# Moving the last three of eight elementwise subtractions per pair from VectorE to GpSimd in a fused embedding, attention and FFN kernel

## The reference, cut to what matters

```python
h = patches @ tokW + tokb, joined with rows of the text table   # 192 tokens per sequence
h = h + attention(layernorm(h))                                 # causal, one head of 256
h = h + ffn(layernorm(h))
# ffn: x_norm = x / rms(x); up to 1024 with ternary weights (-1, 0, 1); exact gelu;
#      again x / rms(x); down to 256 with ternary weights
```

## Time and profile before

| what | value |
|---|---|
| median of 3 runs | 1138.72 us (1138.6 to 1143.58) |
| profiled execution, its own time | 1146.54 us |
| profiled execution, span from first to last instruction | 1144.7 us |
| busy in the span: PE, PEld | 968.9 us (85%), 849.7 us (74%) |
| busy in the span: DVE, ACT, POOL | 895.5 us (78%), 568.8 us (50%), 473.1 us (41%) |
| DMA, mean over the span | 84 GB/s |

### The profile page before, as it was taken

One profiled execution on the slowest core, in us unless ns is written; L12 is line 12 of the kernel. 1 busy time (PEld: TensorE's weight loads), 2 busy tenths in 40 slices (PEclk: granted clock), 3 DMA queues, 4 the chain that ended last, 5 costly groups with the idle time before them and its releaser, 6 DMA issues. The chain is left out here.

```text
span 1144.7 us, 19447 instructions
## 1 busy us (share of the span) xinstructions
PE 968.9 (85%) x5806; PEld 849.7 (74%) x5806; DVE 895.5 (78%) x2534; ACT 568.8 (50%) x1110; POOL 473.1 (41%) x602
## 2 busy tenths in 40 slices
PE   2378799999999999875789999999999999963886
PEld 2377688888888888774367788888888888752776
DVE  1667788888888888865137899998999998854997
ACT  1034555555555555552255577666666766612331
POOL 2124444444444444332023455554454454424443
PEclk9589899999999999986779999999999999955989
DMA  3111111111111110002169999999999999944110
GB/s 133 60 61 38 37 40 41 37 37 37 37 37 37 37 37 25 15 21 85 66 63 119 139 154 151 160 156 133 152 163 152 147 161 125 134 67 142 49 56 19
DMA packets 133534, 96.05 MB, mean 84 GB/s; under 512 B 9672, under 2 KB 127568, under 8 KB 132944
## 3 DMA queue, kind: packets, MB, share of 16 engines
q1 hardware_dynamic: 131920, 90.93, 52.1%
q0 software_dynamic: 1536, 4.20, 1.2%
HBM read 31.66 MB, written 13.11 MB: 39 GB/s over the span
## 5 line engine op out<-in xcount | busy, mean ns | idle before, releaser
L285 POOL TENSOR_TENSOR gelu_lo<-gelu_out,gelu_hi 128x384 fp32r<-128x384 f32 x80 | 87.8, 1105 | 98.8 <-DVE gelu_hi L435 98.8
L562 PE MATMUL psA<-x2T_hi,ternary_up 128*128 128x384 f32 x256 | 92.7, 362 | 11.0 <-ACT gelu_out L351 7.3
L609 PE MATMUL psA<-ternary_down,gelu_hi 128*128 128x256 f32 x384 | 99.0, 295 | 3.2 <-POOL gelu_lo L285 3.2
L846 POOL TENSOR_TENSOR B_decayed_u<-B_scan_in 128x512 f32<-128x512 f32 x48 | 62.1, 1293 | 86.6 <-DMA B_scan_in<-B_stage 79.9
L609 PE MATMUL psA<-ternary_down,gelu_lo 128*128 128x256 f32 x384 | 96.6, 289 | 0.0
L562 PE MATMUL psA<-x2T_lo,ternary_up 128*128 128x384 f32 x256 | 86.0, 336 | 0.0
L1096 PE MATMUL psB<-Win_hi,B_x_hi 128*128 128x512 f32 x192 | 84.3, 439 | 0.0
L834 POOL TENSOR_TENSOR B_y<-B_scan_in,B_states 128x512 f32<-128x512 f32 x48 | 62.0, 1291 | 52.1 <-ACT B_states L901 52.1
L1106 PEld LDWEIGHTS psB<-B_partial_dots,B_minus_same_batch 128*128 128x128 f32 x384 | 67.1, 196 | 21.9 <-DVE B_partial_dots L992 13.6
L1008 DVE SCALAR_TENSOR_TENSOR psB<-B_decayed_u,psB 128x128 f32<-128x128 f32 x192 | 68.0, 354 | 16.0 <-PE psB L1106 15.7
L609 PEld LDWEIGHTS psA<-ternary_down,gelu_hi 128*128 128x128 f32 x384 | 75.9, 198 | 4.4 <-POOL gelu_lo L285 3.9
(11 more groups left out here) (251 smaller groups left out, 3448.4 us busy)
## 6 DMA issues: line engine op xcount, KB each, us to landing
B_scan_in<-B_stage SPq DMA_DIRECT2D x192, 256.0 KB, 7.8
patches<-in_patches SPq DMA_DIRECT2D x16, 384.0 KB, 3.1
B_residual<-layer_out SPq DMA_DIRECT2D x48, 128.0 KB, 5.5
out_dram<-B_residual SPq DMA_DIRECT2D x48, 128.0 KB, 4.6
C_raw<-in_experts SPq DMA_DIRECT2D x8, 768.0 KB, 4.3
layer_out<-residual SPq DMA_DIRECT2D x32, 128.0 KB, 1.8
layer_out<-residual SPq DMA_DIRECT2D x32, 64.0 KB, 2.0
weight_stage<-in_upT SPq DMA_DIRECT2D x1, 1024.0 KB, 5.6
```

What stands on the lines that cost most here:

```text
L285: nc.gpsimd.tensor_tensor(act_l[:, k, :], act[:, k % DEEP, :], act_h[:, k, :].bitcast(F32), ALU.subtract).then_inc(s["ffn_lo"], 1)
L562: last = nc.tensor.matmul(out, a, b, start=(n == 0), stop=(n == len(terms) - 1))
L609: last = nc.tensor.matmul(ps[:, 6 + k // 2, (k % 2) * D:(k % 2 + 1) * D], x[:, c, k * P:(k + 1) * P], dn_w[:, c, :], start=(c == 0 and x i ...
L846: nc.gpsimd.tensor_tensor(lu[:, j % 2], ring[:, j % R_RING, :, LAM, :], ring[:, j % R_RING, :, U, :], ALU.mult).then_inc(s["lu"], 1)
```

## The change

`lo_vector`, the chunks whose low part VectorE makes, becomes empty, so `lo_pool` holds all eight. The instructions at L438 vanish, GpSimd runs L285 three more times per pair, and every wait in `wait_lo` counts on GpSimd's semaphore alone.

```diff
-        lo_vector = (3, 5, 7)
+        lo_vector = ()
         lo_pool = [k for k in range(FC) if k not in lo_vector]
```

## The result

The changed kernel takes 1128.2 us (median of 14 runs, 1120.99 to 1134.47) against 1141.36 for the kernel before (14 runs, 1133.55 to 1146.65). The ratio is 0.989, 95% interval 0.9864 to 0.9915: 1.1% faster. The changed kernel was measured once more on another occasion, with 0.986 (0.9819 to 0.9902). The profiled execution takes 1132.51 us with a span of 1130.7. Forecast were 1125.0 against 1138.72, a ratio of 0.988. The change saves 13.2 us, 13.75 forecast. That 1128.2 lies just above the forecast's own range of 1122 to 1128 comes from the kernel before, which took 2.6 us more in these 14 runs than in the first three. Ratios leave out the executions that took over 1.5% more than the fastest of their kernel, two of ten in the run with chunks 3 and 5 alone (its profile is of one of them) and two of thirteen of the kernel before in the set with (1, 2, 3, 5).

The account below looks back on a forecast made before the run. VectorE was taken to set the pace from chunk 3 on, TensorE following. 14 steps x 1.0 + 0.75 - 1.0 = 13.75 us off the median 1138.72 gave 1125.0; own range 1122 to 1128, overall 1119 to 1140, leaving out h1 held.

Parts of the forecast that it names:

- The bound: In part A's regular pairs, VectorE sets the pace from chunk 3 on and TensorE follows it.
- Whoever asks first holds the other: VectorE and GpSimd reading SBUF: first runs; after release the other needs 0.87 (GpSimd), 0.42 (subtraction or addition), 0.21 us (cast).
- Slot 3: Addition 2, cast 4 and `xT_lo` on VectorE: neither gains nor loses; 0.56 saved and 0.21 pause pay for blocked cast.
- the four places: Trace spots showing VectorE and GpSimd holding each other: low part 7, an addition, the `x_normed` behind it, a cast.
- Chunk 7 just in time: GpSimd finishes chunk 7 at 277.1, TensorE needs it at 277.25: 0.1 us to spare; GpSimd's pause hides the moved work.
- Next to nothing left over: TensorE at x2T gains 1.0 us; VectorE is late next, by some 0.1 us per pair.
- More: Rival, chance 0.05: casts never wait behind GpSimd, TensorE's room caps the gain at 1.44 us per pair: 1119 us.
- The last two pairs: Pair before the last gains 0.75 us at h1; last pair loses 1.0 as TensorE waits for GpSimd's chunk 7.
- 15 steps of 28.1 us: Part A's pairs are regular by `rms_mean`, 106.8 to 528.8 us; one pair's reading stands for 14 full steps.
- GpSimd asks first: Rival, chance 0.16: GpSimd's request holds additions 2 and 3, h1 only 0.56 us earlier per pair: 1131.8 us.
- The blocks eat it all: Rival, chance 0.12: GpSimd's chunk 6 slips between casts 6 and 7, h1 gains nothing: 1139.9 us.
- h1 held: Rival, chance 0.15: h1's scalar counts as a second SBUF read, GpSimd holds h1, 0.53 us late per pair: 1147.9 us.

Follow-up runs that it names:

- 3 and 5 alone: Changed kernel, but chunk 7's low part stays on VectorE, so only chunks 3 and 5 move to GpSimd; ratio to the kernel before 1.0095.
- (1, 2, 3, 5): Changed kernel, but VectorE makes the low parts of chunks 1, 2, 3 and 5; 1119.3 us, ratio 0.9822; repeated 1120.2 us, 0.9821.
- 7 alone: Changed kernel, but low parts 3 and 5 stay on VectorE, so only chunk 7's moves to GpSimd; 1126.15 us, ratio 0.9875.
- GpSimd made late: Changed kernel plus one unused subtraction of the same size on GpSimd right ahead of chunk 7's low part; ratio to the kernel before 0.9899.
- (3, 5, 6, 7): Changed kernel, but VectorE makes the low parts of chunks 3, 5, 6 and 7; ratio to the kernel before 1.0014.
- (2, 3, 5): Changed kernel, but VectorE makes the low parts of chunks 2, 3 and 5, GpSimd the other five; 1122.57 us, ratio 0.9818.

## Why the prediction was right

**The bound.** VectorE sets the pace from chunk 3 on, TensorE follows. The waits for `tT_lo` and `x_normed` L535 went when VectorE's chain got shorter, and that for L494, ahead of chunk 3, stayed at 9.7 us. Shown.

**Whoever asks first holds the other.** The rule held wherever the sum depends on it. It failed at cast 4, where the sum does not (next paragraph). The forecast of 0.21 (cast) and 0.87 (GpSimd) behind a release came out: cast 6 ends at 270.21, 0.23 after GpSimd's chunk 5 (269.98), and that chunk ends 0.86 after addition 3 (269.12). The runs with 7 alone and with 3 and 5 alone gave 26.88 and 28.44 for 26.9 and 28.4. So the two parts of the sum are shown by themselves, +1.30 for chunk 7 and -0.29 for chunks 3 and 5: the whole gain of the change comes from chunk 7, and the other two take 0.27 of it back. That chunk 3 has 0 of this and chunk 5 the rest is read from the trace, not from a run of each: `xT_lo` starts 1.89 behind cast 3, 1.90 before.

**Slot 3.** The total of 0 was right, and the way to it was not. Cast 4 was to be held until 272.15, since chunk 3 had asked first, and passed instead; so the rule taken from the four places is not complete. The forecast stood because `xT_lo` waits for ScalarE either way. Chunk 4 starts 1.92 behind cast 3, 1.98 forecast, which is luck: it was to wait for a held cast 4, and it waited for a chunk 3 that ended late. Cast 5 is held by 0.04 instead of 0.08.

**Chunk 7 just in time.** Forecast 6.85 us behind cast 3, measured 6.84 (272.33 - 265.49). That any lateness would stall TensorE one for one holds for down.0 and not for the period: with chunk 7 about 1 us late the period rose by 0.26.

**What is late next.** "Next to nothing left over" at x2T was too small a room. I took the score matmuls at 2.26 us to the next slot, and with `x_normed` ready they take 2.15, so TensorE still waits 0.17 for `x_normed` in each pair, 0.04 forecast. Behind it comes the wait ahead of ss, which I counted (0.35) for the rival *More* and not here; it measures 0.41. Neither touched the forecast, which VectorE's chain sets.

**The last two pairs** were mis-sized, at -0.25 us together. The steps of `rms_mean` there are 26.08 for 27.49 and 20.33 for 19.49: +1.41 - 0.84 = 0.57. The last one's 1.0 of loss is 0.84. In the pair before it, cast 3 to h1 takes 5.56 for 6.29, a gain of 0.73 as forecast (0.75); the other 0.66 comes from TensorE's clock (last section), which the sum had at nothing.

**The steps.** The sum was 14 x 1.0 - 0.25 = 13.75. The "15 steps of 28.1 us" are a mean over unequal ones: 36.94, twelve of 28.0 to 28.2, 27.49 and 19.49. The twelve middle steps gave 1.0 to 1.04 each, 12.2 together. The one ahead of them gave 0.65 (36.94 to 36.30); it holds a wait of TensorE of some 7 us behind ScalarE, which waits for the transfer of a weight. For the first pair no gain shows: its `rms_mean` stands at 106.8 in both, but over all traces it lies anywhere between 103.4 and 108.5, so that the trace cannot tell. The sum from first to last is 13.45. That the total came so near to 13.75 is in part luck: the regular pairs gave 1.1 less than 14.0, the last two 0.8 more than -0.25.

**The rivals.** GpSimd asks first: no, both additions took 0.55. The blocks eat it all: no, cast 7 ran through behind a held cast 6 (1.44 for both). More: in part, cast 4 did not have to wait, and it brought nothing, as VectorE then waited 0.81 for `xT_hi`. h1 held: no, 0.47 over GpSimd's chunks 6 and 7. One scalar per partition and one tile from SBUF, with the other tile from PSUM, were not held by GpSimd here. The Trainium skill, "SBUF — State Buffer", section "Who interferes with whom", frees instructions with at most one SBUF input, outside the two-port modes, and leaves open whether a scalar counts as one; by this trace it does not.

## What to carry to other kernels

Where two engines hold each other up, counting instructions is not enough; count meetings too, that is, instructions of the two that overlap in time and hold each other. Moving work pays most where the moved instruction stood behind the other engine, and costs where the one that follows it will stand there. Read in order of time which instructions are longer than their shortest form, and what ran beside them: here taking away one subtraction of 1.25 us, 0.69 of it waiting, brought 1.30 per pair, more than the whole gain. A replay of one regular pair from measured starts and ends, with the rule of who waits taken from four places of the same trace, gave the period to 0.02 us here, and to 0.04 in the runs with 7 alone and with 3 and 5 alone. It did less well where other things than VectorE's chain counted or the rule was stretched: 26.55 for 26.4 in the run with (1, 2, 3, 5), and 27.42 for 28.1 where GpSimd was made late.

## What the runs showed of the hardware

In the pair before the last, 0.66 of the 1.41 us gained goes with where TensorE's clock was low. A window over x2T and ss (length, busy times with counts, granted clock, DMA), in the kernel before, behind a wait of 4.15 us for `x_normed`:

```profile
506.60:509.30 2.70, 2.64 (x13) 2.64 (x14) 1.03 (x3) 1.04 (x2) 0.00 (x0) 0.50 0.00 0
```

and in the changed kernel, first over down.0 and down.1 behind three waits for GpSimd (0.49, 0.84 and 0.46 us), then over x2T and ss, behind a wait of 0.95 us:

```profile
488.00:492.00 4.00, 3.72 (x18) 3.46 (x18) 2.48 (x11) 0.00 (x0) 2.29 (x4) 0.61 0.00 0
```

```profile
492.90:495.00 2.10, 1.76 (x13) 1.52 (x14) 1.07 (x4) 1.08 (x2) 0.00 (x0) 1.00 0.00 0
```

In the kernel before the clock was at its lower level (1.2 GHz, 0.50) just where the end of the pair hangs on TensorE. In the changed kernel the low stretch (0.61 in the mean) came earlier, in matmuls whose end nobody waited for, and the clock was full (2.4 GHz, 1.00) over x2T and ss. From x2T to `rms_mean` it took 2.65 us (506.66 to 509.31) and then 1.99 (492.99 to 494.98): 0.66 of the 1.41 us gained in that pair. The second trace of the changed kernel shows the same (2.00), and so do the runs with 7 alone and with GpSimd made late. With 3 and 5 alone and with (3, 5, 6, 7) it is 2.65 at the low clock, but so it is with (2, 3, 5), where chunk 7 is on GpSimd too. That the earlier small waits moved the low stretch is my reading; it was not tried by itself, and the cause stays open.

Between a cast that starts as an addition ends (0.08 ahead of it) and a GpSimd instruction that started 0.39 us before that end, either may win: at cast 4 the cast passed in all 14 regular pairs of the changed kernel, at cast 6 it was held in all of them. The starts in the trace do not tell which it will be.
